# Second attention of a two-layer network: which engine makes a head's low parts, and which one divides by the row sums

## The reference

```
xn = layernorm(x)                      # for the network
xa = layernorm(xn) * gamma + beta      # for the attention
q, k, v = split(xa @ w_qkv)            # 16 heads of 64
q, k = rotate(q), rotate(k)            # by sin and cos of the position
probs = softmax(q @ k.T / 8)           # 2048 x 2048 for each head
x = x + concat(probs @ v) @ w_out + b_out + ffn(xn)
```

## Time and profile before

| | |
|---|---|
| median of 3 runs | 3486.61 us (3481.0 to 3489.35) |
| profiled execution | 3484.36 us, of which 3482.6 us from first to last instruction (the span) |
| busy in the span | PE 3037.7 us (87%), DVE 2877.3 us (83%), ACT 2989.6 us (86%), POOL 2537.8 us (73%) |
| mean granted TensorE clock | 0.872 of full speed |
| from the first exponential of the second attention to its last divide | 2059.92 to 3308.4 us |

### The profile page before, as it was taken

One profiled execution on the slowest core, in us unless ns is written; L12 is line 12 of the kernel. 1 busy time (PEld: TensorE's weight loads), 2 busy tenths in 40 slices (PEclk: granted clock), 3 DMA queues, 4 the chain that ended last, 5 costly groups with the idle time before them and its releaser, 6 DMA issues. The chain is left out here.

```text
span 3482.6 us, 59948 instructions
## 1 busy us (share of the span) xinstructions
PE 3037.7 (87%) x19523; PEld 1275.8 (37%) x19523; DVE 2877.3 (83%) x4324; ACT 2989.6 (86%) x2783; POOL 2537.8 (73%) x1581
## 2 busy tenths in 40 slices
PE   6888888888888888888887968999898889989899
PEld 4222112221222212222223424555555555555547
DVE  7989999999999999999997968878887777888421
ACT  3999999999999999999996846878888888878942
POOL 5888888888888888888875524767777776767850
PEclk9788777887778777887778979999999999999999
DMA  2000000000000000000001550100000110000000
GB/s 75 6 8 7 7 0 7 7 7 7 0 7 7 7 7 0 7 7 7 3 6 40 198 143 19 32 26 26 25 26 26 44 32 26 26 26 25 20 22 13
DMA packets 59522, 85.32 MB, mean 24 GB/s; under 512 B 10065, under 2 KB 45905, under 8 KB 58961
## 3 DMA queue, kind: packets, MB, share of 16 engines
q1 hardware_dynamic: 59344, 82.93, 8.3%
HBM read 52.31 MB, written 30.54 MB: 24 GB/s over the span
## 5 line engine op out<-in xcount | busy, mean ns | idle before, releaser
L1264 POOL TENSOR_TENSOR lo<-pr,hi 128x1024 f16<-128x1024 f32 x384 | 883.1, 2323 | 396.3 <-ACT hi L1438 391.1
L1325 DVE TENSOR_REDUCE mx<-mx_ps 128x1 f32<-128x512 f32 x1024 | 660.6, 683 | 127.7 <-PE mx_ps L1480 123.9
L1453 ACT ACTIVATE pr<-s_ps 128x1024 f32<-128x1024 f32 x512 | 533.2, 1041 | 243.4 <-PE s_ps L1511 189.2
L1438 ACT ACTIVATE hi<-pr 128x1024 f16<-128x1024 f32 x512 | 549.3, 1074 | 0.0
L1480 PE MATMUL mx_ps<-ka,qa 128*128 128x512 f16 x1024 | 376.6, 397 | 128.4 <-DVE mx L1325 98.7
L722 ACT ACTIVATE wt<-wt 128x2048 f32<-128x2048 f32 x256 | 485.2, 1896 | 0.5
L713 ACT ACTIVATE wt<-wt,theta_bias 128x2048 f32<-128x2048 f32 (+2 forms) x160 | 482.4, 3015 | 3.2 <-DVE wt L563 2.7
L501 POOL TENSOR_TENSOR wt<-base,wt 128x1024 f32<-128x1024 f32 x192 | 455.3, 2371 | 16.0
L501 POOL TENSOR_TENSOR wt<-vb,wt 128x1024 f32<-128x1024 f32 x192 | 455.1, 2370 | 16.0
L1530 PE MATMUL pv_ps<-vh,hi 128*128 128x129 f16 x4096 | 434.5, 223 | 10.2 <-ACT sums L1444 3.9
L1530 PE MATMUL pv_ps<-vh,lo 128*128 128x65 f16 x4096 | 420.2, 195 | 0.0
(11 more groups left out here) (210 smaller groups left out, 5046.0 us busy)
## 6 DMA issues: line engine op xcount, KB each, us to landing
qk<-stg SPq DMA_DIRECT2D x6, 2048.0 KB, 10.6
vh<-v SPq DMA_DIRECT2D x16, 520.0 KB, 3.4
qa<-qk SPq DMA_DIRECT2D x16, 512.0 KB, 3.6
ka<-qk SPq DMA_DIRECT2D x32, 256.0 KB, 4.8
v<-v_st SPq DMA_DIRECT2D x3, 2080.0 KB, 7.9
qst<-parts_dram SPq DMA_DIRECT2D x144, 32.0 KB
kst<-parts_dram SPq DMA_DIRECT2D x144, 32.0 KB
qk<-stg SPq DMA_DIRECT2D x4, 1024.0 KB, 8.5
```

The costliest lines, as they stand in the source:

```text
L1264: eng.tensor_tensor(lo[:, i % NHL, :, :], pr_slot(i), hi[:, i % NHL, :, :], ALU.subtract).then_inc(lo_done, 1)
L1325: eng.tensor_reduce(mx4[:, q // NCH, q % NCH:q % NCH + 1], mx_ps[:, q % 2, :], AX.X, ALU.max)\
L1438: eng.activation(hi[:, i % NHL, :, :], pr_slot(i), ACT.Copy).then_inc(hi_done, 1)
L1453: eng.activation(pr_slot(i), s_ps[:, i % 2, :, :], ACT.Exp, scale=SM).then_inc(exp_done, 1)
```

## The change

- In stage_attention1, VectorE makes the low parts of steps 24 to 31 of a head (NLV = 8) instead of steps 3, 7, ... 31; GpSimd makes those of steps 0 to 23 in a row. The number on each engine stays 8 and 24. VectorE's order in a step is now half 1 of step i - 3, then half 0 of step i - 2.
- VectorE's `take` keeps the reciprocal and the addition. The multiplication moves to ScalarE (`divide`): four instructions of 128x64 elements, one for each 128 queries, each with the reciprocal as its scale per partition, at i % 8 = 6, two steps after ScalarE's own `take`, between the exponential and the high part.
- At the end of the last head, VectorE makes the last low parts in a loop, and ScalarE divides last.
- In stage_project1, GpSimd writes xn of tile k behind the low part of the tile's second unit, instead of all 16 first.

```
--- before.py
+++ after.py
@@ -1100,9 +1100,6 @@
                 eng.memset(v_st[:, :, :, :, HD1:HD1 + 1], QS)
                 eng.memset(v_st[:, :, :, :, VN:VW], 0.0).then_inc(consts_ready, 1)
                 eng.wait_ge(scales_ready, 1)
-                for k in range(NT):
-                    eng.tensor_scalar(xn[:, k, :], base[:, k, :], mv[:, k, 0:1], tmp[:, 0, k:k + 1],
-                                      ALU.subtract, ALU.mult).then_inc(xn_ready, 1)
                 for u in range(4 * NT):
 
                     k, b = u // 4, u % 4
@@ -1110,6 +1107,9 @@
                     eng.wait_ge(hi_ready, u + 1)
                     eng.tensor_tensor(dst[:, :, 1, :], ra[:, u % 2, :].rearrange("p (h e) -> p h e", h=HB),
                                       dst[:, :, 0, :], ALU.subtract).then_inc(lo_ready, 1)
+                    if b == 1:
+                        eng.tensor_scalar(xn[:, k, :], base[:, k, :], mv[:, k, 0:1], tmp[:, 0, k:k + 1],
+                                          ALU.subtract, ALU.mult).then_inc(xn_ready, 1)
 
             @block.tensor
             def _(eng):
@@ -1214,7 +1214,8 @@
 
     LOW, SUM = 2, 4
 
-    LV = 4
+    NLV = 8
+    NLG = STEPS - NLV
     with ExitStack() as ctx:
         def t(name, shape, dt=F32):
             return ctx.enter_context(nc.sbuf_tensor(name, shape, dt))
@@ -1247,14 +1248,15 @@
             return 2 * g + par
 
         def on_vector(i):
-            return i % LV == LV - 1
+            return i % STEPS >= NLG
 
         def wait_low(eng, h, i):
 
+            before = h + 1 + i // STEPS
             if on_vector(i):
-                eng.wait_ge(lo_vector, STEPS // LV * (h + 1) + i // LV + 1)
+                eng.wait_ge(lo_vector, NLV * before + i % STEPS - NLG + 1)
             else:
-                eng.wait_ge(lo_gpsimd, STEPS // LV * (LV - 1) * (h + 1) + i // LV * (LV - 1) + i % LV + 1)
+                eng.wait_ge(lo_gpsimd, NLG * before + i % STEPS + 1)
 
         def low(eng, h, i, lo_done):
 
@@ -1359,10 +1361,6 @@
                     eng.reciprocal(rden[:, :].unsqueeze(2), sums[:, :, HD1:HD1 + 1])
                     eng.tensor_tensor(sums[:, :, 0:HD1], sums[:, :, 0:HD1], sums[:, :, HD1 + 1:VN], ALU.add)\
                        .then_inc(div_ready, 1)
-                    eng.wait_ge(div_ready, n_ + 1)
-                    eng.tensor_tensor(attn1[:, c * TS:(c + 1) * TS, bass.ds(h * HD1, HD1)], sums[:, :, 0:HD1],
-                                      rden[:, :].unsqueeze(2).to_broadcast([P, TS, HD1]), ALU.mult)\
-                       .then_inc(attn_ready, 1)
 
                 def low_half(h, i, n_):
 
@@ -1387,7 +1385,7 @@
                             first_row(i // 4)
                         for hq, q in banks[:cut]:
                             reduce_bank(hq, q)
-                        for n_ in range(2):
+                        for n_ in (1, 0):
                             at = i - LOW - n_
                             if (at >= 0 or not first) and on_vector(at):
                                 low_half(h, at, n_)
@@ -1403,8 +1401,10 @@
                         if i % KP == SUM and not (first and i == SUM):
                             take(h - 1 if i == SUM else h, (i // KP - 1) % NS)
                     if last:
-                        for n_ in range(2):
-                            low_half(h, STEPS - 1, n_)
+                        low_half(h, STEPS - LOW - 1, 1)
+                        for i in range(STEPS - LOW, STEPS):
+                            for n_ in range(2):
+                                low_half(h, i, n_)
                         take(h, NS - 1)
 
                 for q in range(NQ1):
@@ -1437,6 +1437,14 @@
                     eng.wait_ge(pv_done, STEPS * (h + 2) + i + 1 - NHL)
                     eng.activation(hi[:, i % NHL, :, :], pr_slot(i), ACT.Copy).then_inc(hi_done, 1)
 
+                def divide(h, c):
+
+                    eng.wait_ge(div_ready, NS * h + c + 1)
+                    for j in range(TS):
+                        last = eng.activation(attn1[:, c * TS + j, bass.ds(h * HD1, HD1)], sums[:, j, 0:HD1],
+                                              ACT.Identity, scale=rden[:, j:j + 1])
+                    last.then_inc(attn_ready, 1)
+
                 def take(h, c):
 
                     eng.wait_ge(attn_ready, NS * h + c + 1)
@@ -1453,11 +1461,14 @@
                         eng.activation(pr_slot(i), s_ps[:, i % 2, :, :], ACT.Exp, scale=SM).then_inc(exp_done, 1)
                         if i % KP == SUM and not (first and i == SUM):
                             take(h - 1 if i == SUM else h, (i // KP - 1) % NS)
+                        if i % KP == SUM + 2 and not (first and i == SUM + 2):
+                            divide(h - 1 if i == SUM + 2 else h, (i // KP - 1) % NS)
                         if i >= 1 or not first:
                             high(h, i - 1)
                     if last:
                         high(h, STEPS - 1)
                         take(h, NS - 1)
+                        divide(h, NS - 1)
 
                 one(0, first=True)
                 with eng.Fori(1, H - 1) as h:
@@ -1568,8 +1579,8 @@
 
 
                 eng.sem_inc(pv_done, 2 * STEPS)
-                eng.sem_inc(lo_vector, STEPS // LV)
-                eng.sem_inc(lo_gpsimd, STEPS - STEPS // LV)
+                eng.sem_inc(lo_vector, NLV)
+                eng.sem_inc(lo_gpsimd, NLG)
                 eng.sem_inc(s_done, 2 * STEPS)
                 eng.sem_inc(mx_taken, 2)
                 eng.sem_inc(mt_copied, 1)
```

18 lines of the change are left out of this document (9 added, 9 removed).

## The result

| | before | after |
|---|---|---|
| median, beside each other | 3483.81 us (3480.99 to 3489.35) | 3430.35 us (3422.39 to 3432.45) |
| ratio | | 0.984, interval 0.9819 to 0.9862 |
| profiled execution (span) | 3484.36 us (3482.6) | 3422.39 us (3420.6) |

The account below looks back on a forecast made before the run. No engine was full; TensorE waited for banks VectorE reduced late, through its order inside a step. From 3484.4 us, -105 (middle heads), -13 (first), +1 (last), -2 (projection) gave 3365 profiled, 3368 predicted; range 3328 to 3420 us.

Parts of the forecast that it names:

- 14 x 68.9: Middle heads of the second attention: 14 heads at 68.9 us each for 76.4, 105 us less.
- What waits behind the moved parts: Around a head's start: the row of maxima comes at 3.2 us, not 4.1, and the 0.9 us keys' wait is covered.
- The multiply leaves VectorE: VectorE's take: moving the multiply removes about 0.5 us of the 1.0 us by which it holds banks up.
- 0.3 us kept for a take: Stall still allowed for each of a head's three takes in bank steps, 3 x 0.3 us.
- second part: Head from step 1's exponential to step 28's: 57.9 us for 65.6, mostly 53.8 us of bank steps.
- The rival on GpSimd: GpSimd's unbroken run of low parts sets every head: 2.5 us a low, 71.8 us a head, 3409 us; chance 0.13.
- Low halves leave the bank steps: VectorE's low halves move to steps 26 to 31 and 0 to 2; of 16, only two stand among banks.
- The part that ScalarE sets: Head from step 28's exponential to the next head's step 1: 9.7 us plus a 1.0 us divide, 10.7 us.
- that rival: Divides on ScalarE bring two table loads each, 1.28 us apiece with drain: 3534 us; chance 0.04, shared with an unseen stall.
- near 88: First head from step 0 to 28: near 88 us, 13 us less, as low halves and two multiplies go.
- the 30 that were named as the sign: Sign of being right: TensorE's wait for VectorE's banks under 30 us in the middle heads.
- The cover of the keys' wait: Step 2 of a head: the divide delays TensorE to 12.2 us, so the 0.9 us wait for keys is covered.

Follow-up runs that it names:

- Experiments 1: The changed kernel with VectorE's loop over pairs of heads written out as straight code; 3395.60 us, ratio 0.9745.
- version 3: The changed kernel with VectorE's loop over single heads in place of pairs; 3391.56 us, ratio 0.973.
- Experiment 8: version 3 with a take's addition made as a reduction over pairs, one input in place of two; 3350.14 us, ratio 0.9608.
- Experiment 10: The kernel before with only the multiplication moved to ScalarE, the old split of low parts kept; 3403.18 us, ratio 0.9745.
- Experiment 14: Experiment 10 with VectorE's loop over single heads and two of a head's five load transfers moved behind the values' transfer; 3398.99 us.
- version 7: version 3 with two of a head's five load transfers moved behind the values' transfer; 3383.15 us, ratio 0.9707.
- (5): version 3 with the multiplication back on VectorE and ScalarE's divides gone; 3574.04 us, ratio 1.0251.
- 11: Experiment 8 with the old split, VectorE making the low parts of every fourth step; 3463.34 us, ratio 0.992.
- Experiments 12: Experiment 10 with the addition made as a reduction of one input, nothing else; 3464.25 us, ratio 0.9937.
- 13: The kernel before with the multiplication four steps later, still on VectorE; 3443.50 us, ratio 0.9868.

## Why the prediction was wrong

The direction was right and the size was not: 3368 forecast, 3430 measured. Against the profiled execution the forecast was 3365, measured 3422.39, 57 us more. The middle heads hold it all: 1023.8 us against 14 x 68.9 = 964.6, 59 us. Of these 41 us are the five heads at a return (391.2 us together against 5 x 70.06), 16 us are 14 x (70.06 - 68.9), and 2 us one head of 72.2. The rest nearly cancels: first head -14.3 (forecast -13), up to the first row -3.0 (forecast -2), and from the last copy of a row to the end 247.6 before and 250.1 after, +2.5 (forecast +1).

**The step that failed first: *What waits behind the moved parts*.** It moved the low halves of 29 to 31 to the start of the next head and asked what the row and the keys see of it, but not what in VectorE's program lies ahead of them there. A return of the loop does, every second head. Its 4 to 6 us had no price, since before they lay in VectorE's idle. Experiments 1 and 3 take it away in two ways and win 35 and 39 us. By the Trainium skill, "Runtime: NRT & Kernel Launch", section Instruction fetch mechanics, a taken branch to a target outside the loaded pages waits until the instructions are fetched by a transfer. The traces agree: in each of the five stalls two packets of instructions go over a queue on which version 3, with a loop over one head and no stall, has none in the middle heads, and VectorE resumes 2.3 to 2.8 us after the second starts. With other transfers moved away it is 2.0 to 2.7 us, and the stall is shorter. Written out, the list takes 10 such packets from 2220 to 3180 us, and no stall stands there.

**The second: *The multiply leaves VectorE*, in its price and in the 0.3 us kept for a take.** The addition stayed at 0.4 us in the sum. Beside GpSimd's unbroken run it lasts 1.3 to 2.1 us among the banks, and TensorE stands up to 1.5 us for it. Experiment 8 takes away the second input and changes little else, and wins 41 us against 3, 2.9 us a usual head. That is more than the 1.2 us that were missing, because the 58.2 us forecast for the second part still had 0.9 us for takes and 0.3 us for other stalls in it. The rival on GpSimd had the right mechanism, and looked at GpSimd's pace alone; it was VectorE that paid. By the Trainium skill, GPSIMD Engine Reference, Key points, the two share their interfaces to SBUF for VectorE's two-input instructions; the trace agrees (up to 2.12 us with two inputs, 0.67 us with one).

**The third: *Low halves leave the bank steps*, as the reason for the gain.** The 7.5 us a head were laid to low halves among banks. Experiment 10 leaves them where they were, and heads fall from 76.4 to 70.1 and 71.5 us (70.6 by the mean). Experiment 14 gives 70.1, the same as the new split in 7. So in the middle heads the split won nothing that the division had not already won, and with the multiplication on VectorE it loses (5). It shortened the first head, where VectorE is the bound, by 10.6 us (14 against 7), and it makes room for the reduction: 3350 us in 8 against 3463 in 11. The rows for the true cause were there: a low half of 2.24 us right behind a take, another of 0.68. The prediction read them as "beside GpSimd or not", and spread the price over all halves. The question was why it was beside GpSimd in that place, and the answer is a multiplication in a pause that had 0.13 us of room without it, at step 12 of each head; behind it TensorE waits, and then works at the lower clock from 2586.56 to 2590.09 us. Experiments 12 and 13 show this from both sides.

**What held.** The part that ScalarE sets, 10.69 us for 10.7; the small instructions, 0.24 us; no loads of tables in the attention, so what one costs with its drain (1.28 us in that rival, where the row shows the load alone) was never put to the test; the low halves, 0.71 us for "near 0.7"; the first head, 86.3 us for "near 88"; GpSimd's run does not bind, at 2.13 us a low part. TensorE's waits for banks, 45.9 us, stayed above the 30 that were named as the sign. The cover of the keys' wait did not always hold: it came back at 0.94 us in four heads of version 3, 8 us in all by version 7.

**Open.** Why a head is 70.1 us in both orders is not settled; with less work in the take the new order reaches 67.2. The share of the projection is below what can be measured.

## What to carry to other kernels

Before work is moved to the start of a loop's body, look at what the engine did there: an idle may hide the loop's own return, and the waits show that price only once something needs the engine; the instruction packets among the DMA queues show it earlier. Where two engines share a path, a duration is not a property of the instruction: ask which one starts first and by how much, since a margin of 0.13 us decided over 60 us. Of a change with two halves, time each: the better half alone was worth 84 us, and the whole 53.

## What the runs showed of the hardware

- A VectorE instruction with two inputs in SBUF that starts while GpSimd runs a 128x1024 subtraction ends only behind it. In the kernel before, all 143 low halves (128x512) that started so ended 0.54 to 0.61 us behind GpSimd's instruction, and all 19 additions (128x256) 0.28 to 0.29 us behind. So the price is what is left of GpSimd's instruction: a half takes 0.68 to 2.60 us (0.68 alone), an addition 1.05 to 1.84 us there and up to 2.12 us in version 3 (0.40 alone). If VectorE starts 0.13 us ahead, it keeps its 0.68 us and GpSimd's takes 2.54 us for 2.13. A reduction of 128x512 with one input stays at 0.67 us beside GpSimd.
- A return of VectorE's loop over two heads cost 4.2 to 6.0 us of standing, behind packets of 8 KB on an instruction queue; one over a single head fetched nothing and cost nothing that the profile shows.
- A scaled copy of 128x64 with a pointer costs ScalarE 0.24 us from start to start in a chain. The estimate that the prediction gives by the Trainium skill, "ScalarE: Activation LUTs", section What ACT_TABLE_LOAD costs, 239 ns, agrees.
